# ScalarE issues the stores of the layer-norm stages, SyncE only the loads

## The chip, the core and the metric

The kernel runs on one core of a Trainium2 chip. The metric is the device time of one execution in microseconds (us). Three runs of the kernel before took 9191.78, 9195.85 and 9219.41 us; the median is 9195.85. All data are f32. A core has TensorE (PE), VectorE (DVE), ScalarE (ACT), GpSimd (POOL) and SyncE (SP), each with its own list of instructions and a sequencer that works through it in order; they wait for each other by semaphores. 16 DMA engines move data between HBM and the on-chip memories.

## The reference, cut to what matters

A graph network in four layers over 50000 nodes of 256 features, with 50000 edges sorted by destination. Each layer adds what its graph operation gives to x and normalises each row:

```python
x = _layernorm(x + _L0_gnn_ref(x, edge_index, edge_weight, L0_gnn_W, L0_gnn_b), axis=-1)
x = _layernorm(x + _L1_gnn_ref(x, ...), axis=-1)   # attention, 8 heads
x = _layernorm(x + _L2_gnn_ref(x, ...), axis=-1)   # attention, 8 heads
x = _layernorm(x + _L3_gnn_ref(x, ...), axis=-1)   # filter, update, batch norm over all nodes, plus x
```

Layer 0 is a two-hop propagation, then relu and a 256 x 256 product. Layers 1 and 2 take softmax-weighted sums over the edges of each destination. Layer 3 has a batch norm over nodes, so its last pass needs the sums of a pass before.

## The kernel before, in words

The nodes are padded to 128 x 392 and laid out so that partition p holds 392 consecutive nodes. A step handles G = 2 columns, that is 2 tiles of 128 rows x 256, and there are NS = 4 buffers of everything; so each phase has 392 / 2 = 196 steps (R = 49 rounds of 4). The program runs twelve phases one after the other: setup, hop_edges, hop_nodes, hop_edges, layer_nodes(0), attention_edges(1), layer_nodes(1), attention_edges(2), layer_nodes(2), filter_edges, update_nodes, finish_nodes. The layer-norm stages are layer_nodes(0), (1), (2) and finish_nodes.

In layer_nodes GpSimd gathers the sums of each node from HBM (L717, two indirect DMAs a step). SyncE loads x (L688), in layer 0 also the table T (L691). VectorE combines them, adds the bias (L728), adds up to z (L779), takes bn_stats (L613) and bn_aggr (L621), and later the reciprocal (L631) and the shift (L636). ScalarE takes the root (L626), and applies scale and shift to make xo (L642). In layers 0 and 1 TensorE turns xo (psX, L831), ScalarE copies it (L801), TensorE multiplies it by the next layer's weights (psV, L858, one bank for each of the two tiles and no second pair), and ScalarE copies the result into tt (L808, L810), the rows of the next layer's gather table. In layer 0 ScalarE also rectifies (L791), and TensorE has a turn (psR) and a product (psZ, L844) more. The two results go to HBM: xo to X1, X2 or X3 (L696), tt to T1 (L702), in layer 1 to T2 and ET (L704, L705).

In finish_nodes SyncE loads ht (L1346, the transposed output of update_nodes) and x (L1348), ScalarE applies the batch norm (L1379), TensorE turns it back (L1365), VectorE adds x (L1405), and the same norm follows, with xo stored to out (L1352).

The order on each engine is written out by unrolled(rounds, slots, stages): at time t it calls every stage of its list, in the order of the list, for step t minus the stage's lag. On SyncE load has lag 0, store lag APPLY + 2 and store_table lag TABLE + 2 (TABLE = APPLY + 2; APPLY is 4 in layer 0, else 2); in finish_nodes load has 0 and store 5. On ScalarE the root has lag ADD (3 in layer 0, else 1), apply has APPLY = ADD + 1, the copy of the turned tile APPLY + 1 and the table rows TABLE. hold(e, sem, value) puts a wait in the engine's list; on SyncE, GpSimd and ScalarE it stands as an instruction of its own. A load holds for the buffers' last readers four steps back (mixed and biased; in layer 0 turned for T; in finish_nodes turned for ht and summed for x). A store holds for the semaphore of what it stores (normed, evened, finished). apply and the table rows hold for the store four steps back (stored, stored_t).

Of the kernel before, what the change touches and what calls it, by code (L numbers as in the profile page):

```python
# [24 lines left out]
SW = VW + H  # L25
TW = SW + H
# [17 lines left out]
def signal(stage, s):  # L44

    sems, _, dmas = stage
    return sems[s if dmas else 0]


def done(stage, i, s, back=0):  # L50

    sems, slots, dmas = stage
    if dmas:
        return sems[(s - back) % slots], (i + ((s - back) // slots + 1)) * (16 * dmas)
    return sems[0], i * slots + (s - back + 1)


def total(stage, rounds):

    sems, slots, dmas = stage  # L60
    return [(sem, rounds * (16 * dmas if dmas else slots)) for sem in sems]


def unrolled(rounds, slots, stages):

    for t in range(rounds * slots + max(lag for _, lag in stages)):
        for stage, lag in stages:
            if 0 <= t - lag < rounds * slots:
                stage((t - lag) // slots, (t - lag) % slots)


def build(nc, N, x, src, srcT, dst, dst_next, ew, rbfT, attr3T, attr64T, w0T, b0, w1T, w1, a1, encW, bias1,
# [28 lines left out]
    def hold(e, sem, value):  # L101


        if isinstance(value, int) and value <= 0:
            return
        e.wait_ge(sem, value)
        if e.engine in alone:
            e.sem_inc(marks, 1)  # L108
# [4 lines left out]
    def nodes(t):  # L113
        return t[0:NP, :].rearrange("(p c) d -> p c d", p=P)
# [3 lines left out]
    T1, T2, ET = dram("T1", NP, TW), dram("T2", NP, SW), dram("ET", NP, H)  # L118
# [4 lines left out]
    with ExitStack() as keep:  # L123
# [524 lines left out]
        def layer_nodes(layer):  # L648

            xin = x if layer == 0 else nodes((X1, X2)[layer - 1])  # L650
            xout = nodes((X1, X2, X3)[layer])
            table = layer < 2
            with ExitStack() as ctx:
                G, NS = 2, 4
                R = C // (G * NS)
# [5 lines left out]
                xT, tt = (tiles("xT", D), tiles("tt", TW)) if table else (None, None)  # L661
# [18 lines left out]
                with nc.Block() as block:  # L680
                    @block.sync
                    def _(e):

                        def load(i, s):
                            c = bass.ds(i * (G * NS) + s * G, G)
                            hold(e, *done(st_["mixed"], i, s, NS))
                            hold(e, *done(st_["biased"], i, s, NS))
                            e.dma_start(xt[s][:], xin[:, c, :]).then_inc(signal(loaded, s), 16)  # L688
                            if layer == 0:
                                hold(e, *done(st_["turned"], i, s, NS))  # L690
                                e.dma_start(yt[s][:], nodes(T)[:, c, :]).then_inc(signal(loaded, s), 16)  # L691

                        def store(i, s):
                            c = bass.ds(i * (G * NS) + s * G, G)
                            hold(e, *done(st_["normed"], i, s))
                            e.dma_start(xout[:, c, :], xo[s][:]).then_inc(signal(stored, s), 16)  # L696

                        def store_table(i, s):
                            c = bass.ds(i * (G * NS) + s * G, G)
                            hold(e, *done(st_["evened"], i, s))  # L700
                            if layer == 0:
                                e.dma_start(nodes(T1)[:, c, :], tt[s][:]).then_inc(signal(stored_t, s), 16)  # L702
                            else:
                                e.dma_start(nodes(T2)[:, c, :], tt[s][:, :, 0:SW]).then_inc(signal(stored_t, s), 16)  # L704
                                e.dma_start(nodes(ET)[:, c, :], tt[s][:, :, SW:TW]).then_inc(signal(stored_t, s), 16)  # L705

                        unrolled(R, NS, [(load, 0), (store, APPLY + 2)] + ([(store_table, TABLE + 2)] if table else []))
                        for sem, value in total(stored, R) + (total(stored_t, R) if table else []):
                            e.wait_ge(sem, value)

                    @block.gpsimd
                    def _(e):
# [74 lines left out]
                    @block.scalar  # L787
                    def _(e):
                        def rectify(i, s):
                            hold(e, *done(st_["mixed"], i, s))  # L790
                            e.activation(yt[s][:], yt[s][:], ACT.Relu, scale=0.5).then_inc(signal(st_["rectified"], s), 1)  # L791

                        def copy_turned(i, s):
                            hold(e, *done(st_["turned"], i, s))
                            hold(e, *done(st_["product"], i, s, NS))
                            e.copy(rT[s][:].rearrange("p g d -> p (g d)"), psR[s % 2][:]).then_inc(signal(st_["copied"], s), 1)

                        def copy_turned_x(i, s):
                            hold(e, *done(st_["turnedx"], i, s))
                            hold(e, *done(st_["tabled"], i, s, NS))  # L800
                            e.copy(xT[s][:].rearrange("p g d -> p (g d)"), psX[s % 2][:]).then_inc(signal(st_["copiedx"], s), 1)  # L801

                        def tabled_rows(i, s):

                            hold(e, *done(st_["tabled"], i, s))
                            hold(e, *done(stored_t, i, s, NS))
                            for k in range(G):
                                e.copy(tt[s][:, k, 0:VW].rearrange("p (h w) -> p h w", h=H)[:, :, 0:HD],  # L808
                                       psV[k][:, 0:D].rearrange("p (h d) -> p h d", h=H))
                                ins = e.copy(tt[s][:, k, VW:TW], psV[k][:, D:DW])  # L810
                            ins.then_inc(signal(st_["evened"], s), 1)

                        def apply(i, s):
                            hold(e, *done(stored, i, s, NS))
                            if table:
                                hold(e, *done(st_["turnedx"], i, s, NS))
                            ln_apply(e, i, s, st_["normed"])

                        stages = [(rectify, 0), (copy_turned, TURN)] if layer == 0 else []
                        stages += [(lambda i, s: ln_root(e, i, s), ADD), (apply, APPLY)]  # L820
                        if table:
                            stages += [(copy_turned_x, TURNX), (tabled_rows, TABLE)]
                            e.wait_ge(ones, 1)
                        unrolled(R, NS, stages)

                    @block.tensor
                    def _(e):
# [499 lines left out]
        def finish_nodes():  # L1327
            with ExitStack() as ctx:
# [11 lines left out]
                with nc.Block() as block:  # L1340
                    @block.sync
                    def _(e):

                        def load(i, s):
                            hold(e, *done(turned, i, s, NS))
                            e.dma_start(ht[s][:], HT[:, :, bass.ds(i * (G * NS * P) + s * (G * P), G * P)]).then_inc(signal(loaded, s), 16)  # L1346
                            hold(e, *done(summed, i, s, NS))
                            e.dma_start(xt[s][:], nodes(X3)[:, bass.ds(i * (G * NS) + s * G, G), :]).then_inc(signal(loaded, s), 16)  # L1348

                        def store(i, s):  # L1350
                            hold(e, *done(finished, i, s))
                            e.dma_start(out[:, bass.ds(i * (G * NS) + s * G, G), :], xo[s][:]).then_inc(signal(stored, s), 16)  # L1352

                        unrolled(R, NS, [(load, 0), (store, 5)])
                        for sem, value in total(stored, R):
                            e.wait_ge(sem, value)

                    @block.tensor
                    def _(e):
# [10 lines left out]
                    @block.scalar  # L1370
                    def _(e):
                        e.wait_ge(agged, 1)
                        e.activation(sd[:, :, 0], mv[:, :, 1], ACT.Sqrt, bias=epsc[:]).then_inc(rooted, 1)
                        e.wait_ge(scaled, 4)

                        def batch_norm(i, s):
                            hold(e, *done(loaded, i, s))
                            for m in range(K):
                                ins = e.activation(ht[s][:, m, :], ht[s][:, m, :], ACT.Identity, bias=shift[:, m, :], scale=scale[:, m, :])  # L1379
                            ins.then_inc(signal(normed, s), 1)  # L1380

                        def apply(i, s):
                            hold(e, *done(stored, i, s, NS))
                            ln_apply(e, i, s, finished)

                        unrolled(R, NS, [(batch_norm, 0), (lambda i, s: ln_root(e, i, s), 2), (apply, 3)])

                    @block.vector
                    def _(e):
# [77 lines left out]
```

## Time and profile before

| | us |
|---|---|
| median of 3 runs | 9195.85 |
| profiled execution | 9210.81 |
| its span, first to last instruction | 9209.1 |
| TensorE busy | 4799.2 (52%) |
| VectorE busy | 6234.8 (68%) |
| ScalarE busy | 3278.4 (36%) |
| GpSimd busy | 5451.7 (59%) |
| layer_nodes(0), 1962 to 2876 | 914 |
| layer_nodes(1), 4057 to 4835 | 778 |
| layer_nodes(2), 5890 to 6492 | 602 |
| finish_nodes, 8663 to the end | 546 |

The shares are over the whole span, and the phases have different limits, so what an engine does in one phase is to be read from that phase. PE is TensorE's matmuls, PEld its weight loads; the ends of matmuls are modelled, so their starts tell more. SPq is SyncE's sequencer with its DMA issues. "[1.79 <-DMA xt<-X]" behind an instruction is the idle time of its engine just before, and what ended it. The DMA share is the mean busy share of the 16 DMA engines.

### The profile page before, as it was taken

The page shows a single profiled execution, that of the slowest core. Times are in us where ns is not written, and L with a number is a line of the kernel's source. Part 1 is how long each engine was busy: PE and PEld are TensorE (multiplying, and loading weights), DVE is VectorE, ACT ScalarE, POOL GpSimd, SP SyncE. Part 2 cuts the span into 40 slices and gives each one's busy share as a digit, 9 for nine tenths or more (in the row PEclk, how much of TensorE's full clock was granted, in tenths as well). Part 3 has the DMA queues.
Part 4 walks back from the last instruction along what each step waited for, and adds up shares of the span by engine and source line. Part 5 has one row for each costly group of instructions (what it writes and reads, how often), then busy time and mean ns, then how long its engine had stood idle before and what let it go on. Part 6 is the DMA issues. An engine that isn't in the chain of part 4 may idle for free. (4 is left out here: it accounts for less than half of the span.)

```text
span 9209.1 us, 103278 instructions
## 1 busy us (share of the span) xinstructions
PE 4799.2 (52%) x18908; PEld 3452.2 (37%) x18908; DVE 6234.8 (68%) x20123; ACT 3278.4 (36%) x8442; POOL 5451.7 (59%) x5121
## 2 busy tenths in 40 slices
PE   8856000039996333347771111100688887899743
PEld 4422000038884211225551111100455555788622
DVE  7899333358887999977777777799544444455566
ACT  4433002347774111126660000144222222344588
POOL 7877777764445666655547777677788888100000
PEclk9999555569997555569995555555777778899855
DMA  0299899989886445459984444588544444566688
GB/s 20 99 344 338 284 309 297 309 274 299 297 294 195 146 146 148 147 173 285 278 268 117 122 122 123 165 266 266 108 79 79 79 79 79 165 200 199 214 292 284
DMA packets 1143019, 1839.84 MB, mean 200 GB/s; under 512 B 218094, under 2 KB 564898, under 8 KB 1142374
## 3 DMA queue, kind: packets, MB, share of 16 engines
q1 hardware_dynamic: 884838, 1245.79, 39.8%
q0 software_dynamic: 257536, 587.44, 26.3%
q14 instruction: 483, 3.96, 0.1%
q8 instruction: 162, 2.65, 0.1%
HBM read 1044.55 MB, written 788.03 MB: 199 GB/s over the span
## 5 line engine op out<-in xcount | busy, mean ns | idle before, releaser
L717 POOL DMA_INDIRECT st<-S,last_i x1176 | 1325.6, 1127 | 897.6 <-DVE yt L759 370.4
L915 POOL DMA_INDIRECT rows<-T,src_i x784 | 800.8, 1021 | 251.1 <-issue 248.1
L642 ACT ACTIVATE xo<-z,shift,rsd 128x256 f32<-128x256 f32 x1568 | 851.0, 591 | 1.3 <-issue 1.1
L1128 POOL DMA_INDIRECT A<-comb,ai x392 | 702.5, 1792 | 159.6 <-issue 145.0
L931 PE MATMUL psE<-encs,attr 4*128 4x256 f32 x784 | 404.9, 668 | 745.2 <-DMA attr<-in_attr3T 745.2
L946 ACT ACTIVATE ex<-diff 128x32 f32<-128x32 f32 x392 | 89.8, 229 | 1709.6 <-DVE diff L993 1709.6
L1200 DVE TENSOR_SCALAR eq<-psI,src_f 128x128 f32<-128x128 f32 x392 | 136.7, 349 | 743.2 <-DMA A<-comb,ai 708.4
L931 PE MATMUL psE<-fes,attr 64*128 64x8 f32 x784 | 199.5, 363 | 821.7 <-DMA attr<-in_attr64T 819.4
L477 DVE SCALAR_TENSOR_TENSOR sums<-sums,same,rows 128x256 f32<-128x256 f32 x784 | 380.2, 485 | 326.6 <-ACT rows L458 312.4
L1142 PE MATMUL psH<-rbf,wf1s 20*128 20x256 f32 x784 | 278.9, 485 | 613.9 <-DMA rbf<-in_rbfT 613.9
L931 PEld LDWEIGHTS psE<-encs,attr 4*128 4x128 f32 x784 | 227.5, 319 | 922.3 <-DMA attr<-in_attr3T 884.7
L613 DVE BATCH_NORM_STATS2 row_stats<-z 128x6 f32<-128x256 f32 x1568 | 560.6, 399 | 0.1
L913 POOL DMA_INDIRECT rowsd<-T,dst_i x392 | 384.1, 980 | 266.3 <-DVE sums L1010 150.3
L543 PE MATMUL psC<-sums,chain 128*128 128x256 f32 x4 | 2.4, 699 | 1034.9 <-PEq L417 1034.9
L1156 PE MATMUL psF<-wf2s,hid 128*128 128x256 f32 x1568 | 522.2, 494 | 0.0
L858 PE MATMUL psV<-w2s,xT 128*128 128x272 f32 x1568 | 436.5, 424 | 122.5 <-ACT tt L810 122.5
L931 PEld LDWEIGHTS psE<-fes,attr 64*128 64x128 f32 x784 | 181.2, 319 | 840.4 <-DMA attr<-in_attr64T 838.0
L458 ACT ACTIVATE rows<-rows,w_next 128x256 f32<-128x256 f32 x392 | 177.6, 500 | 850.8 <-DMA rows<-T,src_i 850.8
L445 POOL DMA_INDIRECT rows<-in_x,src_i x392 | 375.6, 958 | 170.0 <-issue 151.8
L1121 POOL DMA_INDIRECT rows<-X,dst_i x392 | 391.3, 998 | 135.9 <-issue 119.1
L913 POOL DMA_INDIRECT rowsd<-ET,dst_i x392 | 376.9, 962 | 150.3 <-issue 119.2
L445 POOL DMA_INDIRECT rows<-T,src_i x392 | 382.1, 975 | 127.7 <-issue 101.2
(232 smaller groups left out, 15612.8 us busy)
## 6 DMA issues: line engine op xcount, KB each, us to landing
X<-xo SPq DMA_DIRECT2D x588, 256.0 KB
xt<-X SPq DMA_DIRECT2D x588, 256.0 KB
S<-sums SPq DMA_DIRECT2D x392, 272.0 KB, 2.4
A<-zero SPq DMA_DIRECT2D x392, 256.0 KB, 4.8
S<-sums SPq DMA_DIRECT2D x392, 256.0 KB, 4.1
xt<-in_x SPq DMA_DIRECT2D x392, 256.0 KB
T<-tt SPq DMA_DIRECT2D x196, 280.0 KB
T<-tt SPq DMA_DIRECT2D x196, 272.0 KB
```

Of the source, the lines that this page charges most:

```text
L445: e.indirect_dma_start(rows[s][:, k, :], None, table, bass.IndirectOffsetOnAxis(ap=src_i[:, c:c + 1], axis=0))\
L477: ins = e.scalar_tensor_tensor(sums[s][:, k, 0:D], last, same[:, bass.ds(i * (G * NS) + (s * G + k), 1)], rows[s][:, k, :], ALU.mult, ALU.add)
L613: ins = e.bn_stats(row_stats[s][:, k, :], z[s][:, k, :])
L642: ins = e.activation(y[s][:, k, :], z[s][:, k, :], ACT.Identity, bias=shift[s][:, k, :], scale=rsd[s][:, k, :])
L717: e.indirect_dma_start(st[s][:, k, :], None, sums_table, bass.IndirectOffsetOnAxis(ap=last_i[:, c:c + 1], axis=0))\
L858: mm = e.matmul(psV[k][:, 0:DW], xT[s][:, k, m * P:(m + 1) * P], weights[:, m, :], start=m == 0, stop=m == K - 1)
L913: e.indirect_dma_start(rowsd[s][:, k, :], None, dtable, bass.IndirectOffsetOnAxis(ap=dst_i[:, c:c + 1], axis=0))\
L915: e.indirect_dma_start(rows[s][:, k, :], None, table, bass.IndirectOffsetOnAxis(ap=src_i[:, c:c + 1], axis=0))\
L931: mm = e.matmul(psE[s % 2][:, k * EW:(k + 1) * EW], attr[s][:, k, :], weights[:], start=True, stop=True)
L1121: e.indirect_dma_start(rows[s][:, k, :], None, X3, bass.IndirectOffsetOnAxis(ap=dst_i[:, c:c + 1], axis=0))\
L1128: e.indirect_dma_start(A[k], bass.IndirectOffsetOnAxis(ap=ai[s][:, k, :], axis=0), comb[s][:, k, :], None, compute_op=ALU.add).then_inc(si ...
L1156: mm = e.matmul(psF[s % 2][:, k * D:(k + 1) * D], hid[s][:, m, k * P:(k + 1) * P], wf2s[:, m, :], start=m == 0, stop=m == K - 1)
```

## The change

The stores and their closing waits move from SyncE's list to ScalarE's. On ScalarE, store has lag APPLY + 1 and stands behind apply, and store_table has lag TABLE + 1 and stands behind the table rows; in finish_nodes store has lag 4 and stands behind apply (lag 3). What a store waits for was thus made by ScalarE in its iteration before. SyncE keeps the loads with their waits. The numbers of DMAs, their sizes, buffers and semaphores are the same.

```diff
 # layer_nodes, block.sync
-                        def store(i, s):
-                            c = bass.ds(i * (G * NS) + s * G, G)
-                            hold(e, *done(st_["normed"], i, s))
-                            e.dma_start(xout[:, c, :], xo[s][:]).then_inc(signal(stored, s), 16)
-
-                        def store_table(i, s):
...
-                        unrolled(R, NS, [(load, 0), (store, APPLY + 2)] + ([(store_table, TABLE + 2)] if table else []))
-                        for sem, value in total(stored, R) + (total(stored_t, R) if table else []):
-                            e.wait_ge(sem, value)
+                        unrolled(R, NS, [(load, 0)])
 # layer_nodes, block.scalar
+                        def store(i, s):
+                            c = bass.ds(i * (G * NS) + s * G, G)
+                            hold(e, *done(st_["normed"], i, s))
+                            e.dma_start(xout[:, c, :], xo[s][:]).then_inc(signal(stored, s), 16)
+
+                        def store_table(i, s):
+                            c = bass.ds(i * (G * NS) + s * G, G)
+                            hold(e, *done(st_["evened"], i, s))
+                            if layer == 0:
+                                e.dma_start(nodes(T1)[:, c, :], tt[s][:]).then_inc(signal(stored_t, s), 16)
+                            else:
+                                e.dma_start(nodes(T2)[:, c, :], tt[s][:, :, 0:SW]).then_inc(signal(stored_t, s), 16)
+                                e.dma_start(nodes(ET)[:, c, :], tt[s][:, :, SW:TW]).then_inc(signal(stored_t, s), 16)
+
                         stages = [(rectify, 0), (copy_turned, TURN)] if layer == 0 else []
-                        stages += [(lambda i, s: ln_root(e, i, s), ADD), (apply, APPLY)]
+                        stages += [(lambda i, s: ln_root(e, i, s), ADD), (apply, APPLY), (store, APPLY + 1)]
                         if table:
-                            stages += [(copy_turned_x, TURNX), (tabled_rows, TABLE)]
+                            stages += [(copy_turned_x, TURNX), (tabled_rows, TABLE), (store_table, TABLE + 1)]
                             e.wait_ge(ones, 1)
                         unrolled(R, NS, stages)
+                        for sem, value in total(stored, R) + (total(stored_t, R) if table else []):
+                            e.wait_ge(sem, value)
 # finish_nodes, block.sync
-                        unrolled(R, NS, [(load, 0), (store, 5)])
+                        unrolled(R, NS, [(load, 0)])
 # finish_nodes, block.scalar
-                        unrolled(R, NS, [(batch_norm, 0), (lambda i, s: ln_root(e, i, s), 2), (apply, 3)])
+                        unrolled(R, NS, [(batch_norm, 0), (lambda i, s: ln_root(e, i, s), 2), (apply, 3), (store, 4)])
+                        for sem, value in total(stored, R):
+                            e.wait_ge(sem, value)
```

## Rows read from the trace of the kernel before

**Rows 1.** Windows of the four stages: us, busy per engine, PEclk, DMA share, GB/s

```profile
1962.00:2876.00 914.00, 885.52 (x4704) 750.41 (x4704) 753.46 (x2356) 679.48 (x1960) 432.01 (x393) 0.99 0.87 288
4057.00:4835.00 778.00, 550.20 (x2352) 393.85 (x2352) 584.90 (x2156) 503.53 (x1566) 428.02 (x391) 0.94 0.90 275
5890.00:6492.00 602.00, 0.00 (x0) 0.00 (x0) 580.19 (x2156) 255.88 (x589) 462.60 (x390) 0.50 0.84 261
8663.00:9209.10 546.10, 218.36 (x784) 140.29 (x784) 344.96 (x1378) 437.82 (x982) 0.00 (x0) 0.50 0.86 283
```

**Rows 2.** SyncE's waits over the whole span: total us, times, longest

```profile
SPq L108 <- ACT xo L642: 1135.7, 734, 7.6
...
SPq L108 <- ACT tt L810: 361.3, 389, 2.8
...
SPq L108 <- DVE z L766: 13.4, 2, 7.0
```

**Rows 3.** Groups by line, in 4200:4700 and in 8750:9150 (columns as in the page)

```profile
L728 DVE TENSOR_TENSOR xb<-xt,b1s 128x512 f32<-128x512 f32 x128 | 88.7, 693 | 119.4 <-DMA xt<-X 118.8
...
L1379 ACT ACTIVATE ht<-ht,shift,scale 128x256 f32<-128x256 f32 x296 | 160.7, 590 | 70.5 <-DMA xt<-X 69.5
```

**Rows 4.** Windows inside two stages, and one outside (columns as in rows 1)

```profile
460.00:690.00 230.00, 136.46 (x345) 58.49 (x346) 213.93 (x690) 78.04 (x174) 163.83 (x171) 1.00 1.01 344
4200.00:4700.00 500.00, 359.99 (x1534) 258.15 (x1534) 381.49 (x1408) 327.47 (x1023) 279.55 (x255) 0.95 0.91 279
8750.00:9150.00 400.00, 165.24 (x595) 106.06 (x593) 251.85 (x1038) 329.51 (x742) 0.00 (x0) 0.50 0.89 292
```

**Rows 5.** Timeline in layer_nodes(1): start us, us, engine, line, operation

```profile
4401.97 0.20 ACT L810 COPY tt<-psV 128x16 f32<-128x16 f32 x1
...
4402.25 0.37 SPq L704 DMA_DIRECT2D T<-tt  x1
...
4402.31 2.07 PE L858 MATMUL psV<-w2s,xT 128*128 128x272 f32 x8 [0.60 <-ACT tt L810]
...
4402.67 0.47 SPq L705 DMA_DIRECT2D ET<-tt  x1
...
4403.33 0.35 SPq L688 DMA_DIRECT2D xt<-X  x1
...
4405.53 2.07 PE L858 MATMUL psV<-w2s,xT 128*128 128x272 f32 x8 [0.72 <-ACT tt L810]
...
4407.49 0.69 DVE L728 TENSOR_TENSOR xb<-xt,b1s 128x512 f32<-128x512 f32 x1 [1.79 <-DMA xt<-X]
```

**Rows 6.** Timeline in finish_nodes: SyncE's issues and ScalarE

```profile
9042.79 1.07 ACT L1379 ACTIVATE ht<-ht,shift,scale 128x256 f32<-128x256 f32 x2
...
9042.97 0.34 SPq L1352 DMA_DIRECT2D out<-xo  x1
...
9044.05 0.54 SPq L1348 DMA_DIRECT2D xt<-X  x1
...
9045.05 1.09 ACT L1379 ACTIVATE ht<-ht,shift,scale 128x256 f32<-128x256 f32 x2
...
9046.05 0.28 ACT L626 ACTIVATE sd<-mean_var,epsc 128x2 f32<-128x2 f32 x1
...
9046.23 1.08 ACT L642 ACTIVATE xo<-z,shift,rsd 128x256 f32<-128x256 f32 x2
...
9048.19 1.09 ACT L1379 ACTIVATE ht<-ht,shift,scale 128x256 f32<-128x256 f32 x2 [0.88 <-DMA xt<-X]
```

**Rows 7.** Timeline in layer_nodes(0), TensorE: one group in two steps

```profile
2402.45 0.60 PE L831 MATMUL psR<-ident,yt 128*128 128x128 f32 x4
...
2406.89 0.60 PE L831 MATMUL psR<-ident,yt 128*128 128x128 f32 x4
```

**Rows 8.** DMA issues of the page: count, KB each, median us from issue to landing

```profile
out<-xo SPq DMA_DIRECT2D x196, 256.0 KB, 3.4
...
st<-S,last_i POOLq DMA_INDIRECT x1568, 4.5
```

More of the change, by code:

```diff
@@ L691, in load @@
                                 e.dma_start(yt[s][:], nodes(T)[:, c, :]).then_inc(signal(loaded, s), 16)
-                        def store(i, s):
-                            c = bass.ds(i * (G * NS) + s * G, G)
-                            hold(e, *done(st_["normed"], i, s))
-                            e.dma_start(xout[:, c, :], xo[s][:]).then_inc(signal(stored, s), 16)
-                        def store_table(i, s):
[L699 to L705, printed above, removed]
-                        unrolled(R, NS, [(load, 0), (store, APPLY + 2)] + ([(store_table, TABLE + 2)] if table else []))
-                        for sem, value in total(stored, R) + (total(stored_t, R) if table else []):
-                            e.wait_ge(sem, value)
+                        unrolled(R, NS, [(load, 0)])
                     @block.gpsimd
@@ L1348, in load @@
                             e.dma_start(xt[s][:], nodes(X3)[:, bass.ds(i * (G * NS) + s * G, G), :]).then_inc(signal(loaded, s), 16)
-                        def store(i, s):
-                            hold(e, *done(finished, i, s))
-                            e.dma_start(out[:, bass.ds(i * (G * NS) + s * G, G), :], xo[s][:]).then_inc(signal(stored, s), 16)
-                        unrolled(R, NS, [(load, 0), (store, 5)])
-                        for sem, value in total(stored, R):
-                            e.wait_ge(sem, value)
+                        unrolled(R, NS, [(load, 0)])
                     @block.tensor
@@ L1384, in apply, with store @@
                             ln_apply(e, i, s, finished)
-                        unrolled(R, NS, [(batch_norm, 0), (lambda i, s: ln_root(e, i, s), 2), (apply, 3)])
+                        def store(i, s):
+                            hold(e, *done(finished, i, s))
+                            e.dma_start(out[:, bass.ds(i * (G * NS) + s * G, G), :], xo[s][:]).then_inc(signal(stored, s), 16)
+                        unrolled(R, NS, [(batch_norm, 0), (lambda i, s: ln_root(e, i, s), 2), (apply, 3), (store, 4)])
+                        for sem, value in total(stored, R):
+                            e.wait_ge(sem, value)
                     @block.vector
```

## The prediction

> **What bounds the kernel now.** I read the times of the four changed stages first, then whom SyncE's queue waits for, then one step of each stage in order of time. The changed stages, called 0, 1, 2 and final here, take 914, 778, 602 and 546 us [rows 1], 2840 of the 9209 us; the other eight phases stay as they are. Each stage has 196 steps of two 128-row tiles.
>
> SyncE's waits say who holds the loads back [rows 2]: 1135.7 us in all for ScalarE's normalised tile and 361.3 for its table rows. For what an x load itself needs in stages 1 and 2 (the add to z that frees its buffer, L766) it waits twice in all, 13.4 us, once a stage, in the fill. So the buffer is free long before; the load stands in the queue behind a store whose data is not made yet. That costs where the load is then late. In 500 us of stage 1 (128 steps, 3.906 us each) VectorE idles 118.8 us for the x tile; in 400 us of the final stage (296 activations, so 148 steps, 2.703 each) ScalarE idles 69.5 us for its loads [rows 3].
>
> Stage 1, one step [rows 5]. ScalarE's last table copy ends at 4402.17; SyncE issues the two table stores (0.37 and 0.47 us), and the load at 4403.33; VectorE can use it at 4407.49, 4.16 us after. By the queue's order the load of step t+1 stands behind the table store of step t-6, which ScalarE makes in its iteration t-2 (the table rows lag by 4), so the way round spans three steps: copy to load issue 1.16, load 4.16, VectorE's iteration 381.49/128 = 2.98 [rows 4], ScalarE's iteration about 3.2 (the pitch of TensorE's psV, to which its copies keep). That is 11.5 us, 3.83 a step, and measured is 3.906. The stall is this loop.
>
> The final stage is a loop of the same kind [rows 6]: the out store is issued at 9042.97, the xt load behind it at 9044.05, and ScalarE starts on it at 9048.19. With 2.27 us for its iteration that is 7.5 us for three steps here; on the mean 8.1. When its loads are there a step takes 2.26 (9042.79 to 9045.05).
>
> Stage 0 is another case: TensorE starts its group psR at 2402.45 and 2406.89 [rows 7], 4.44 us apart, and it is busy 885.5 of 914 us [rows 1]. 196 x 4.44 = 870, the rest is fill and drain. TensorE is the bound, and the buffers make up for a late load. In stage 2 VectorE is busy 580.2 of 602 us [rows 1]; no load or store touches that.
>
> **The change, part by part.**
> *SyncE loses the stores*: 588 X stores, 196 table stores in stage 0 and 392 in stage 1, 196 of out, each 0.34 to 0.47 us of issue [rows 5, 6], and their waits. Now a load follows its own buffer. In stage 1 that is VectorE's mix of four steps back: four periods less one VectorE iteration, 4 x 3.3 - 3 = 10 us, for 4.2 us of flight. In the final stage xt waits for the add of four steps back, which comes after TensorE's turn and the root of another step, by the code some 3.5 us into that ScalarE iteration: 4 x 2.26 - 3.5 = 5.5 us for the 4.1 of flight. Enough, if flights don't grow much.
>
> *What is late next in stage 1.* TensorE's psV starts at 4402.31 and 4405.53, both times as ScalarE's copies out of the same banks end [rows 5]: 3.22 us a step. The other bound is the DMA engines, share 0.91 at 279 GB/s [rows 4]. As these transfers are, they need 0.91 x 3.906 = 3.55 us a step. The window 460:690 shows share 1.01 and 344 GB/s with another mix of sizes; at that rate the 279 x 3.906 = 1090 KB of a step take 3.17. So the new step ends between 3.22 and 3.55, if all goes, and 3.906, if nothing does. I take 3.4, and 0.1 for lateness that stays: (3.906 - 3.5) x 196 = 80 us; bounds 0 and 134.
>
> *The final stage.* ScalarE's floor is 2.26. DMA as it is: 0.89 x 2.703 = 2.40; at 344 GB/s 789 KB take 2.29. With both so near to each other, and xt's slack short, I take the upper one: (2.70 - 2.40) x 196 = 59 us; bounds 0 and 87.
>
> *Stages 0 and 2.* Stage 0 has 914 - 870 = 44 us besides TensorE's pace, most of it fill and drain (the pipeline is nine steps deep in the table store): 8 us. Stage 2 has 22 us besides VectorE's work, part of it loads: 8. Bounds for the two together 0 and 25.
>
> *ScalarE gains the stores*: one a step in stage 2 and the final one, two in stage 0, three in stage 1, each with a wait on its own step before (long there) and a mark. The trace before has no DMA issued on ScalarE. By SyncE's rows an issue is 0.34, 0.37 and 0.47 us. The two ends: nothing, if the sequencer is ahead of its engine, or all of it. For ahead: the output activation stands behind waits that follow the root in the list, and yet starts at 9046.23, before the root that started at 9046.05 with 0.28 us is over [rows 6]; so the waits were read while the engine worked. The X and out stores stand behind two activations of 1.08 us together, which hide 0.34. In stage 1 the two table stores (0.84, with waits about 1.05) stand behind table copies that I put at 0.8 of the 3.22 - 2.07 = 1.15 us between two psV groups, so 0.25 us shows. ScalarE's other work of a step, 327.47/128 = 2.56 [rows 4] less 0.8, is 1.8, and with 0.25 it fits into psV's 2.07, by a hair. I take nothing for the issues; the row that shows the sequencer ahead is nearest.
>
> The Trainium skill speaks against this cover. "Perfetto Trace Analysis", DMA Instruction — HWDGE, has the issuing sequencer itself wait, have the descriptors made, and only then be free for its next instruction. No row before shows ScalarE in that state. By that rule and with no work queued ahead, the sum would be that of the rival "issue shows".
>
> *A store goes out later*: behind the next activation pair, up to one step. Its buffer is wanted again four steps on, so three are left, 3 x 2.26 = 6.8 us in the final stage, for 3.4 us to landing [rows 8]. Nothing.
>
> Sum: 80 + 59 + 8 + 8 = 155. The profiled execution took 9210.8 (span 9209.1), so 9056; the median of the runs, 9195.85, is 15 lower, so 9041.
>
> **The rivals.**
> *Next wait in line (0.17).* With the loads early VectorE waits for the gathers: two of about 1.1 us on GpSimd (279.55/255 [rows 4]) plus 4.5 to landing [rows 8] plus a VectorE iteration, about 10 us for four periods of 3.2 to 3.5. Against it: 3 us of slack, and no idle for st in stage 1 now. For it: DMA engines near full make flights longer. Stage 1 then stays near 3.75, 31 us: 31 + 59 + 16 = 106, time 9090.
>
> *DMA is at its limit now (0.12).* The share is 0.84 to 0.90 in all four stages [rows 1]; if that is what a mix of loads, stores and gathers yields, a deeper prefetch only lengthens flights. Against it: 1.01 is reached elsewhere [rows 4]. Gain 16 from stages 0 and 2 or less: 9180. The Trainium skill says it in "DMA: Bandwidth & Descriptors", Issuing engines are not separate DMA queues: DMAs of several issuers share the same 16 DMA engines, and only issue time is saved. Rows 2 show waiting, which that sentence leaves out.
>
> *Issue shows, slower (0.09).* If ScalarE stands still while it issues, stage 1 needs 2.56 + 1.18 (0.34, 0.37, 0.47) + 0.35 for waits = 4.1 a step, 0.2 x 196 = +39. Final: 329.51/148 = 2.23 + 0.34 + 0.1 = 2.67, and part of the load wait stays, +15. Stage 0: 679.48/196 = 3.47 + 0.68 + 0.2 = 4.35 of 4.44, TensorE sometimes unfed, +6. Sum +60: 9255. It decides from 1.34 us a step in stage 1, ScalarE's idle time now.
>
> *All floors reached (0.07).* 3.22, 2.26, 4.44: 134 + 86 + 8 + 12 = 240, time 8956.
>
> **How the numbers follow.** The forecast has 0.55, its own range is 9000 to 9085. The range for 8 in 10 is 8970 to 9185: it holds the forecast, the next wait and the DMA rival's middle, not the slower case. A difference under 0.3% (28 us) can't be told from none. Faster: 0.55 + 0.17 + 0.07 = 0.79; same: 0.12; slower: 0.09.
>
> **What would show it.** After the change: SyncE waits for VectorE and TensorE (mix, z, psN) alone; VectorE's idle for xt in stage 1 is under 20 us in 500, ScalarE's in the final stage under 30 in 400; the DMA share is 0.95 or more in both; stages 0 and 2 are within 15 us of 914 and 602; ScalarE has no idle time ended by "issue". It is wrong if stage 1 stays over 3.8 a step with xt early, if activations beside a store start 0.3 us or more after their inputs, or if the DMA share stays at 0.90.

## The result and the profile after

The changed kernel takes 8955.74 us (median of 4 runs, 8954.23 to 8959.3); the kernel before took 9193.82 beside it. The ratio is 0.9737, with a 95% interval from 0.9718 to 0.9755. The forecast was 9041 with a range from 8970 to 9185, so the direction was right and the time lies below the range, at the fourth rival ("all floors reached", 8956, given 0.07). The profiled execution has a span of 8952.5 us, 256.6 less than before.

The windows of the four stages, and one inside stage 1 and one inside the final stage, columns as in [rows 1]:

```profile
1960.80:2846.70 885.90, 869.17 (x4680) 746.97 (x4681) 755.87 (x2352) 674.03 (x1947) 488.96 (x392) 0.99 0.91 295
4034.20:4682.50 648.30, 492.90 (x2331) 375.75 (x2332) 589.78 (x2156) 511.64 (x1556) 476.70 (x392) 0.98 1.01 328
5742.70:6332.00 589.30, 0.00 (x0) 0.00 (x0) 573.18 (x2156) 254.66 (x589) 455.24 (x392) 0.50 0.89 267
8508.00:8952.50 444.50, 218.20 (x784) 140.07 (x784) 336.88 (x1377) 427.09 (x981) 0.00 (x0) 0.50 0.98 343
...
4100.00:4600.00 500.00, 389.00 (x1848) 296.26 (x1847) 462.70 (x1694) 403.53 (x1232) 375.83 (x308) 1.00 1.03 336
8550.00:8900.00 350.00, 176.15 (x633) 112.93 (x632) 268.99 (x1109) 343.91 (x792) 0.00 (x0) 0.50 1.02 357
```

The DMA share of stage 1 has gone from 0.91 to 1.03 and that of the final stage from 0.89 to 1.02 [rows 4]. To compare stages between kernels I take from each trace the time from the start of the first gather to the start of the last output activation, which makes xo (final stage: from the first output activation to the last), and the mean distance of two steps' output activations:

| | stage 0 | stage 1 | stage 2 | final |
|---|---|---|---|---|
| before, us | 899.8 | 770.6 | 602.4 | 523.7 |
| changed, us | 885.3 | 647.8 | 588.7 | 430.5 |
| before, us a step | 4.48 | 3.87 | 3.01 | 2.68 |
| changed, us a step | 4.41 | 3.25 | 2.94 | 2.21 |
| gain forecast, us | 8 | 80 | 8 | 59 |
| gain measured, us | 14.5 | 122.8 | 13.7 | 93.2 |

These are 244 of the 256.6 us. The other 12 lie outside these stretches, at most 6 us in any one place, and I count them as scatter between executions; no run shows what they are.

SyncE's waits after the change, in the form of [rows 2]:

```profile
SPq L108 <- DVE z L750: 1015.3, 384, 7.1
SPq L108 <- PE psR L831: 653.6, 192, 3.5
...
SPq L108 <- PE psN L1359: 184.4, 188, 9.5
...
SPq L108 <- DVE z L1405: 44.6, 184, 0.7
```

The waits for ScalarE's xo and tt are gone. SyncE now waits at nearly every step for the buffer itself: VectorE's use of it in stages 1 and 2, TensorE's transposes in stages 0 and final. These waits are long (1015 us in stages 1 and 2 alone), which is what a loader that is ahead looks like. They cost next to nothing: the groups that answer to [rows 3], in 4100:4600 and 8550:8900, show no idle time for xt in stage 1 and 5.2 us in the final stage.

```profile
L712 DVE TENSOR_TENSOR xb<-xt,b1s 128x512 f32<-128x512 f32 x154 | 105.1, 682 | 0.0
...
L1373 ACT ACTIVATE ht<-ht,shift,scale 128x256 f32<-128x256 f32 x317 | 171.1, 586 | 6.1 <-DMA xt<-X 5.2
```

One step of stage 1 in order of time, ACTq being ScalarE's sequencer:

```profile
4300.34 0.37 ACT L792 COPY tt<-psV 128x256 f32<-128x256 f32 x1
4300.50 0.41 ACTq L814 DMA_DIRECT2D T<-tt  x1
4300.61 0.18 ACT L794 COPY tt<-psV 128x16 f32<-128x16 f32 x1
4300.67 0.39 ACT L792 COPY tt<-psV 128x256 f32<-128x256 f32 x1
4300.94 0.20 ACT L794 COPY tt<-psV 128x16 f32<-128x16 f32 x1
4300.94 0.52 ACTq L815 DMA_DIRECT2D ET<-tt  x1
4301.25 1.67 PEld L858 LDWEIGHTS psV<-w2s,xT 128*128 128x128 f32 x8 [0.91 <-issue]
4301.28 2.07 PE L858 MATMUL psV<-w2s,xT 128*128 128x272 f32 x8 [0.70 <-ACT tt L794]
4301.59 0.30 ACT L626 ACTIVATE sd<-mean_var,epsc 128x2 f32<-128x2 f32 x1 [0.45 <-issue]
4301.86 0.60 ACT L642 ACTIVATE xo<-z,shift,rsd 128x256 f32<-128x256 f32 x1
4301.99 0.34 ACTq L806 DMA_DIRECT2D X<-xo  x1
4302.37 0.58 ACT L642 ACTIVATE xo<-z,shift,rsd 128x256 f32<-128x256 f32 x1
...
4304.50 2.07 PE L858 MATMUL psV<-w2s,xT 128*128 128x272 f32 x8 [0.71 <-ACT tt L794]
```

The T store is issued (4300.50 to 4300.91) while the copies of a later step run on ScalarE (4300.34 to 4301.14), and the X store while xo is made. Only the tail of ET sticks out: the root starts 0.45 us after the last copy. psV starts at 4301.28 and 4304.50, again 3.22 us apart, and that is the step that half of the stage keeps to (the middle half of its steps take 3.18 to 3.27 us; the mean is 3.25).

### The profile page after: what moved, and what is told of

The parts are those of the page before. It is cut to its first block and busy times, and to the rows that moved or that the text cites. A ratio compares the mean times of both kernels' runs of the same rounds, so it can differ in the third digit from the quotient of the medians.

```text
span 8952.5 us, 103278 instructions
## 1 busy us (share of the span) xinstructions
PE 4724.6 (53%) x18908; PEld 3435.4 (38%) x18908; DVE 6238.9 (70%) x20123; ACT 3276.4 (37%) x8442; POOL 5545.9 (62%) x5121
## 3 DMA queue, kind: packets, MB, share of 16 engines
q8 instruction: 162, 2.65, 0.1%
## 5 line engine op out<-in xcount | busy, mean ns | idle before, releaser
L701 POOL DMA_INDIRECT st<-S,last_i x1176 | 1421.0, 1208 | 650.3 <-issue 316.4
L915 POOL DMA_INDIRECT rows<-T,src_i x784 | 802.6, 1024 | 251.0 <-issue 248.6
L858 PE MATMUL psV<-w2s,xT 128*128 128x272 f32 x1568 | 407.8, 403 | 136.1 <-ACT tt L794 136.1
L583 POOL DMA_INDIRECT st<-S,last_i x392 | 384.0, 980 | 123.4 <-issue 105.7
```

The lines of the kernel that those rows point to most:

```text
L583: e.indirect_dma_start(st[s][:, k, :], None, S0, bass.IndirectOffsetOnAxis(ap=last_i[:, c:c + 1], axis=0))\
L701: e.indirect_dma_start(st[s][:, k, :], None, sums_table, bass.IndirectOffsetOnAxis(ap=last_i[:, c:c + 1], axis=0))\
L858: mm = e.matmul(psV[k][:, 0:DW], xT[s][:, k, m * P:(m + 1) * P], weights[:, m, :], start=m == 0, stop=m == K - 1)
L915: e.indirect_dma_start(rows[s][:, k, :], None, table, bass.IndirectOffsetOnAxis(ap=src_i[:, c:c + 1], axis=0))\
```

## The experiments

The runs went to three chips. On one, the first chip from here on, the kernel before takes 9213 us and the changed one 8961, close to the 9194 and 8956 of the result; on the two others the kernel before takes 9564 to 9576. The difference lies mainly outside the four stages: the first gather of stage 0 stands at 1956 us on the first chip and at 2148 on another, and between stages 1 and 2 (attention_edges(2)) pass 1060 us on the one and 1230 on the other. Yet stage 1 of the changed kernel too is 648 us on the first and 667 to 675 on the others. Its steps there keep their middle (3.23 us for 3.22), but more of them are long: a twentieth take over 4.5 us in c1, over 3.8 in c2 on the first chip. Stages 0 and 2 and the final one agree within some 5 us. So a run is compared with those on the same chip, and each ratio is to the kernel before on that chip. The kernel before was profiled in the trace of the prediction alone. An estimate for the chip of e1 to e7: what these runs spend outside the four stages (6755 to 6782 us), taken from the kernel before beside them, leaves 2784 to 2809 us for its stages, where the trace of the prediction has 2797; so its stage times are used there too. The table has the stages in us as above; each comes from one profiled execution.

| run | ratio, 95% | stage 0 | 1 | 2 | final |
|---|---|---|---|---|---|
| changed (c1) | 0.9756 (0.9736 to 0.9776) | 884.8 | 675.0 | 591.6 | 431.2 |
| e1 waits only | 0.9967 (0.9952 to 0.9983) | 901.4 | 736.3 | 604.3 | 528.2 |
| e2 late on SyncE | 0.9747 (0.9730 to 0.9763) | 884.4 | 665.4 | 594.1 | 419.9 |
| e3 one step later | 0.9755 (0.9736 to 0.9775) | 884.7 | 685.5 | 583.3 | 426.5 |
| e4 tables on SyncE | 0.9921 (0.9904 to 0.9937) | 902.1 | 770.8 | 590.2 | 433.5 |
| e5 two pairs | 0.9777 (0.9761 to 0.9794) | 885.2 | 681.4 | 589.8 | 431.0 |
| e6 one extra | 0.9773 (0.9753 to 0.9792) | 884.9 | 686.5 | 591.8 | 432.8 |
| e7 three extra | 1.0004 (0.9992 to 1.0017) | 886.5 | 812.3 | 597.2 | 501.9 |
| changed (c2), first chip | 0.9721 (0.9708 to 0.9734) | 884.1 | 648.2 | 588.1 | 434.3 |
| e11 final late on SyncE | 0.9708 (0.9694 to 0.9721) | 885.4 | 647.9 | 590.1 | 423.0 |
| e9 less moved | 0.971, one run | 884.9 | 648.1 | 592.3 | 419.7 |
| e10 less moved, two pairs | 0.968, one run | 884.5 | 591.8 | 590.9 | 433.9 |
| changed (c3), third chip | 0.9770 (0.9756 to 0.9784) | 884.8 | 667.3 | 593.3 | 430.7 |
| e13 two pairs again | 0.9796 (0.9781 to 0.9811) | 884.8 | 686.8 | 594.9 | 433.1 |
| e12 pairs and final | 0.9793 (0.9775 to 0.9810) | 885.2 | 684.6 | 595.7 | 422.6 |

**Is it the place of the waits?** e1 is the changed kernel, and SyncE waits as before, without issuing:

```diff
-                        unrolled(R, NS, [(load, 0)])
+                        def await_store(i, s):
+                            hold(e, *done(st_["normed"], i, s))
+
+                        def await_table(i, s):
+                            hold(e, *done(st_["evened"], i, s))
+
+                        unrolled(R, NS, [(load, 0), (await_store, APPLY + 2)] + ([(await_table, TABLE + 2)] if table else []))
```

and in the final stage (await_store, 5) on finished. 

> The changed kernel, with the stores on ScalarE, but SyncE's list gets back the waits that its stores had (for normed, evened and finished, at the old lags) without issuing anything there. Theory (the loads stood behind waits): the old loop is back, less some 1 us of issue out of three steps in stage 1, so stage 1 about 3.6 to 3.8 us a step, the final stage 2.5 to 2.65, the whole 9110 to 9180 us. Rival (what helped is a second issuer with a queue of its own): stays at 8956, 3.25 and 2.2 us a step.

Measured: stages 0, 2 and final are back at 901, 604 and 528 us, the values before. The final stage's 2.71 us a step lies above the 2.5 to 2.65 expected: it got back all of the old loss (2.68), although SyncE issues a DMA less a step. Stage 1 is at 736, 3.70 us a step. Two rows of this kernel, SyncE's waits and the group of the bias add in 550 us:

```profile
SPq L108 <- ACT xo L642: 1131.8, 578, 8.0
```

```profile
L718 DVE TENSOR_TENSOR xb<-xt,b1s 128x512 f32<-128x512 f32 x148 | 102.4, 692 | 105.2 <-DMA xt<-X 81.6 <-issue 23.0
```

The waits alone, with every store on ScalarE, make the loads late again. In stage 1 a part stays gained (3.70 for 3.87). I put it down to the table stores' 0.84 us of issue, which is no longer in a way round of three steps (that would be 0.28 a step, and 0.17 came); no run separates it. The whole time, 9535, is above the 9180 of the expectation because the chip is another; its ratio of 0.9967 is 9163 us where the kernel before takes 9194.

e2 keeps all DMAs on SyncE and raises only the stores' lags:

```diff
-                        unrolled(R, NS, [(load, 0), (store, APPLY + 2)] + ([(store_table, TABLE + 2)] if table else []))
+                        unrolled(R, NS, [(load, 0), (store, APPLY + 5)] + ([(store_table, TABLE + 5)] if table else []))
...
-                        unrolled(R, NS, [(load, 0), (store, 5)])
+                        unrolled(R, NS, [(load, 0), (store, 7)])
```

> The kernel before, all DMAs on SyncE, only the lags of its stores raised: store APPLY+2 to APPLY+5, store_table TABLE+2 to TABLE+5, in the final stage 5 to 7, so that what a store waits for is long made when the list comes to it. Theory (the place of the waits): 8950 to 8990 us, stage 1 near 3.25 a step, the final stage 2.2 to 2.3. Rival (a second issuer and queue are needed, SyncE's issue time or its one queue limits): over 9100.

Measured: 0.9747, the changed kernel's ratio (0.9756 beside it, c1). The final stage takes 2.15 us a step, better than the 2.2 to 2.3 expected. The same group now never idles:

```profile
L728 DVE TENSOR_TENSOR xb<-xt,b1s 128x512 f32<-128x512 f32 x166 | 113.1, 681 | 0.0
```

So neither a second issuer nor its queue is needed. Only the loads must not stand behind waits for work that is later than they are. e3 does the same with one step more of lag (APPLY + 3, TABLE + 3, 6). 

> The kernel before, all DMAs on SyncE, its stores only one step later: lags APPLY+3, TABLE+3 and 6 for APPLY+2, TABLE+2 and 5. Theory (a loop that spans a number of steps): the way round of 11.5 us in stage 1 spans four steps and not three, 2.9 a step, so something else is the bound already, 3.3 to 3.4; the final stage 8.1/4 = 2.0, so 2.15 to 2.2. Almost the whole gain, ratio 0.972 to 0.978. Rival (each step of lag takes off its share): stage 1 about 3.6, ratio near 0.985.

Measured: 0.9755, as good as c1 in the whole. Stage 1 takes 3.44 us a step, just over the 3.3 to 3.4 expected, and 685.5 us for c1's 675.0: VectorE still idles 33.4 us in 550 for xt. So one step just suffices, as a way round over four steps in place of three makes it.

e4 leaves the table stores on SyncE at TABLE + 2 and the X and out stores on ScalarE. 

> The changed kernel, but the table stores (T1, T2, ET) stay on SyncE at their old lag; the X and out stores are on ScalarE. Theory: the loop of stage 1 goes through the table rows, so stage 1 stays at 3.7 to 3.9 us a step; stage 2 and the final stage keep their gain (14 and 93 us); the whole 9070 to 9090. Rival (each store moved gives its share): stage 1 about 3.55, the whole near 9020.

Measured: stages 0 and 1 at 902 and 771 us, their times before; 2 and final at 590 and 434, as changed. VectorE waits for x in stage 1 again, in 550 us:

```profile
L723 DVE TENSOR_TENSOR xb<-xt,b1s 128x512 f32<-128x512 f32 x143 | 99.0, 693 | 125.2 <-DMA xt<-X 113.8 <-issue 10.9
```

Moving the X store alone gives stage 1 nothing: the way round goes through the table rows. Whether moving the table stores alone would give all of it was not run. The whole gained less than expected: 0.9921 (0.9904 to 0.9937), where 9070 to 9090 us would be 0.987 to 0.989. The stages of the profiled run, the fastest of four, account for 100 us of gain, the medians for 75; the rest stays open.

**Does ScalarE pay for issuing?** c1 is the changed kernel on the chip of these runs. 

> The changed kernel once more, on the chip of the runs beside it, as their base. Ratio to before 0.97 to 0.98; stage 0 about 885 us, stage 1 about 648, stage 2 about 589, the final stage 2.2 us a step. If stage 1 takes 665 us or more here, the slower stage 1 of the run with two pairs of psV banks was the chip and not the banks.

Its stage 1 is 675 us, so most of what e5 (two pairs of psV banks, below: 681 us) showed beside 648 was the chip. e6 adds to each X and out store a small one:

```diff
                             e.dma_start(xout[:, c, :], xo[s][:]).then_inc(signal(stored, s), 16)
+                            for j in range(1):
+                                e.dma_start(nodes(SPARE[layer * 1 + j])[:, i * (G * NS) + s * G, :], zero[:, 0:H]).then_inc(spared, 16)
```

> The changed kernel with one more DMA a step on ScalarE behind each X and out store: 128 rows of 32 bytes of zeros to a spare table, 4 KB, no wait. Theory (issue runs beside ScalarE's engine, and there is room in its sequencer): stages 0, 2 and final within 1% of the changed kernel; stage 1, where the issues already hold back the root by 0.45 us a step, 3.3 to 3.5 a step for 3.25. Rival (issue shows): about 0.3 us a step in every stage but 2, some 180 us.

Measured: stages 0, 2 and final unchanged (432.8 for 431.2 us in the final stage), stage 1 686.5 for 675.0, 3.44 us a step as expected. e7 has range(3). 

> As the run with one extra DMA, but three more a step (about 1 us of issue). Theory: the sequencer of ScalarE runs out of room: stage 1 about 4.0 to 4.3 us a step, the final stage 2.15 to 2.6, stage 0 4.5 to 4.8, stage 2 as it was; the whole 200 to 350 us over the changed kernel. Rival (issue never shows beside the engine): under 30 us over it.

Measured: the whole gain is gone (1.0004). Stage 1 takes 4.09 us a step, the final stage 2.57. Stage 0 hides nearly all (886.5 us, 4.41 a step, where 4.5 to 4.8 was expected). ScalarE's groups in 400 us of the final stage:

```profile
L1378 ACT ACTIVATE ht<-ht,shift,scale 128x256 f32<-128x256 f32 x312 | 170.2, 592 | 47.5 <-issue 47.5
```

and one stretch of it in order of time:

```profile
9303.17 0.52 ACTq L1389 DMA_DIRECT2D SPARE<-zero  x1
9303.53 0.58 ACT L643 ACTIVATE xo<-z,shift,rsd 128x256 f32<-128x256 f32 x1
9303.72 0.52 ACTq L1389 DMA_DIRECT2D SPARE<-zero  x1
9304.37 0.60 ACT L1378 ACTIVATE ht<-ht,shift,scale 128x256 f32<-128x256 f32 x1 [0.25 <-issue]
```

So the issues run beside ScalarE's engine, up to a limit. In the final stage one issue more a step (0.82 us of issue in all) fits beside 2.15 us of activations, and three more (1.85 us in all) don't: 0.30 us a step of idle time ended by "issue" (47.5 us in 156 steps). 1.85 is still less than 2.15. I take it that the waits and activations in the sequencer's list, which have no time of their own in the profile, use the rest; no run shows it. The Trainium skill says in "Perfetto Trace Analysis", DMA Instruction — HWDGE, that the sequencer is free for its next instruction only when the issue is done. The trace agrees: the issue at 9303.17 ends at 9303.69, the next starts at 9303.72. What that costs is another matter: the out store's 0.34 us alone are hidden.

**What bounds the stages now?** e9 is the changed kernel without the x loads after the first round, in stage 1 and the final stage; e10 leaves them out in stage 1 alone and has two pairs of psV banks. The outputs of both are not the reference's, and each ran once. The first part of the diff is in both, the rest in e10:

```diff
 # layer_nodes, load on SyncE
+                            if layer == 1 and i:
+                                return
...
 # psV
-                psV = [bank(f"psV{j}", 512) for j in range(2)] if table else None
+                psV = [bank(f"psV{j}", 512) for j in range(4 if layer else 2)] if table else None
+                pairs = 2 if layer else 1
...
-                            hold(e, *done(st_["evened"], i, s, 1))
+                            hold(e, *done(st_["evened"], i, s, pairs))
```

Expected of c2 (the changed kernel beside them), e9 and e10, in this order:

> The changed kernel as the base of the three runs beside it, on their chip. Ratio to before 0.972 to 0.978; the final stage 2.2 us a step, stage 1 between 3.25 and 3.4.

> The changed kernel with the x loads left out after the first round of four steps in stage 1 and in the final stage (so its output is not the reference's): 256 KB a step less, a quarter of stage 1's traffic and a third of the final stage's. If the DMA engines bind (share 1.0), stage 1 falls below 3.2 or steadies, and the final stage below 2.15 us a step. If ScalarE binds the final stage, it stays at 2.15 to 2.2; if TensorE's and ScalarE's cycle binds stage 1, it is 3.22 in nearly every step.

> The changed kernel with two pairs of psV banks and, in stage 1, without the x loads after the first round (its output is not the reference's). If with less moved the psV cycle is what is left (3.22), the second pair now takes it to 2.9 to 3.1 us a step. If GpSimd's gather issue binds (two of 1.2 and 0.3 a step), it stays at 3.0 to 3.2.

Measured, beside c2 (windows 4100:4600, then 8550:8900, of e9; then the first of e10):

```profile
4100.00:4600.00 500.00, 390.78 (x1856) 297.43 (x1855) 464.11 (x1701) 405.81 (x1235) 375.06 (x310) 1.00 0.88 257
8550.00:8900.00 350.00, 181.10 (x650) 116.27 (x651) 276.13 (x1137) 349.57 (x813) 0.00 (x0) 0.50 0.82 244
```

```profile
4100.00:4600.00 500.00, 436.15 (x2040) 316.35 (x2040) 494.55 (x1868) 428.65 (x1359) 392.00 (x341) 1.00 0.93 282
```

With a quarter less to move (257 for 337 GB/s) stage 1 takes 648.1 us for 648.2. The DMA engines do not bind it at a share of 1.03. With the second pair as well it takes 591.8, 2.96 a step, VectorE at 494.6 of 500: the psV cycle (TensorE's product waits until ScalarE has copied the one before out of the same banks) was the bound. In the final stage ScalarE is busy 349.6 of 350 us, and a step is 2.15, its floor. The 2.21 to 2.23 of the changed kernel are 0.06 to 0.08 more; its rows count 5.2 us of idle time for xt in 158 steps, 0.03 a step, and the rest I put down to the same lateness.

With all of the traffic the second pair does not pay. It stands in e5, beside c1; in e13, beside c3; and in e12, which also has the late out store of e11 below. Expected of e5, c3, e13 and e12, in this order:

> The changed kernel with two pairs of psV banks in stage 1 in place of one, so that TensorE's product of a step no longer waits for ScalarE's copies of the step before. If stage 1 (3.25 us a step) is now bound by that cycle of 3.22, it falls to what GpSimd and VectorE need, 3.0 to 3.17, 15 to 40 us off 8956. If it is bound by the DMA engines (share 1.03) or by GpSimd's gathers, it stays within 10 us.

> The changed kernel as the base of the two runs beside it. Stage 1 about 648 us on one kind of chip, about 675 on the other.

> Two pairs of psV banks in stage 1 with all of the traffic, beside the changed kernel. If the DMA engines can carry a step's 1090 KB in less than 3.22 us, stage 1 falls below the changed kernel's, to 3.05 to 3.2 us a step (10 to 40 us off). If their bound is about 3.25 (share 1.03 now), stage 1 stays within 8 us of it.

> Two pairs of psV banks and the final stage's store late on SyncE. Expected: the sum of the two, 10 us for the final stage plus what the run beside it gains in stage 1; 8905 to 8950 where the changed kernel takes 8960.

Measured: stage 1 at 681 us beside 675, and 687 and 685 beside 667; the ratios are 0.9777 beside 0.9756, and 0.9796 and 0.9793 beside 0.9770. No gain came in any of the three. e5's 6 us more is inside the 10 that was to speak for the DMA engines or the gathers as the bound, which e9 and e10 contradict on the first chip; e13's 20 us more fits neither of its two cases; e12 was to gain and takes 30 us more in the median, though its final stage gained 8 us. The steps no longer have 3.22 us each: in e13 a twentieth are under 2.35 and a twentieth over 5.9. The group of the table copies in 500 us, c3 and then e13:

```profile
L792 ACT COPY tt<-psV 128x256 f32<-128x256 f32 x302 | 109.2, 382 | 28.9 <-PE psV L858 11.5 <-DMA srow<-PARTS 5.7 <-issue 5.3
```

```profile
L793 ACT COPY tt<-psV 128x256 f32<-128x256 f32 x292 | 105.1, 380 | 81.3 <-PE psV L859 43.7 <-DMA srow<-PARTS 28.1 <-issue 9.0
```

In this place the only DMA that the copies wait for is the table store of four steps before (the name in the row is of an earlier phase's tensor). So, as I read it, the steps bunch and then stand for stores in flight; that this makes the stage slower is argued from these rows and not shown. Why it makes the mean longer, and whether it would on the first chip, where this was not run, stays open.

**A better version.** e11 is the changed kernel with the out store of the final stage back on SyncE, (store, 7). 

> The changed kernel, but in the final stage the out store is back on SyncE, with lag 7 in place of 5; the layer stages are as changed. The run with all stores late on SyncE had 420 us from the first to the last output activation there, the changed kernel 431. Expected 10 us under the changed kernel beside it (0.1%), if it is the stores' place that makes the difference; none if it was chance.

Measured: 8948.90 us (8945.01 to 8950.61) beside 8960.67 (8952.18 to 8964.26), 11.8 us less, and the final stage 423.0 for 434.3 us. It is the best kernel of this study with the right output, by 0.13%. ScalarE idles 1.7 us in 8550:8900 for xt, beside 8.3 in c2. e12 shows the same 423 us for the final stage on another chip, beside 431 (c3). So the out store costs some 10 us more on ScalarE than late on SyncE; most of it shows in the rows as waits for x and none as issue, and why x comes later stays open.

## Why the prediction was wrong, by its steps

- **SyncE's loads stand behind stores**: right. e1 and e2 show it from both sides, and e4 that stage 1's way round goes by the table rows, as [rows 5] were read; in stage 0 too the gain goes by them (902 us in e4).
- **The loop of three steps**: right in kind. e3's one step more takes it away.
- **Stage 1, "I take 3.4, and 0.1 for lateness that stays"**: this is the term that failed; 3.25 came out, 123 us for 80. It is half of the 85 us by which the forecast was off. The lower bound of 3.22 [rows 5] was the answer. The upper, 0.91 x 3.906 = 3.55 us of DMA work, was none. Two shares of queues, 4200:4700 before (x128 steps) and 4100:4600 after (x154 steps), show why; q0 are the gathers, q1 and q10 the rest:

```profile
q1 hardware_dynamic: 106366, 103.63, 63.2%
q0 software_dynamic: 12258, 35.57, 27.8%
```

```profile
q10 hardware_dynamic: 105594, 84.31, 50.9%
q0 software_dynamic: 14780, 42.90, 26.9%
q1 hardware_dynamic: 22162, 40.36, 24.8%
```

  Loads and stores took 0.632 x 3.906 = 2.47 us a step before and (0.509 + 0.248) x 3.247 = 2.46 after. The gathers took 1.09 before and 0.87 after, with the same bytes. So a gather's busy time is not fixed by its bytes. I read the part that shrank with the step as waiting; the rows show only that it shrank. And e9 shows that even 1.03 was no bound.
- **The final stage, "I take the upper one"**: the same error, 93 us for 59. 0.89 x 2.703 = 2.41 us of share became 1.02 x 2.21 = 2.25. ScalarE's floor was the bound, 2.15 and not 2.26: I had read a step with a short wait in it, and the one before it took 2.17 (9040.62 to 9042.79). e2 keeps to 2.15 with all of the traffic, at a share of 1.03.
- **Stages 0 and 2**: 14.5 and 13.7 us for 8 and 8. In stage 0 the reading was wrong: the 4.44 of [rows 7] was one pair of steps and not the pace. Before, nine steps in ten took 3.8 to 6.0 us, 4.48 in the mean; now most take 4.44, 4.41 in the mean. The 44 us "besides TensorE's pace" were partly such late steps, and 0.075 us a step is the whole gain; the time from the first gather to the first output activation stayed at 25 us. In stage 2 VectorE's 2.91 is reached in most steps.
- **Issues on ScalarE cost nothing**: right within some 10 us, wrong in one sign to look for. ScalarE idles 71.2 us in 500 ended by "issue" in stage 1, 0.46 a step for the 0.25 that I put; psV's 2.07 us cover it, for the step is still psV's 3.22. The out store's place costs the 10 us of e11, and in stage 1 e2, with no store on ScalarE, takes 665 us beside c1's 675, one trace of each.
- **Next wait in line, the gathers**: VectorE idled 0.3 us in 500 for st. The rival is refuted on the chip of the prediction.
- **DMA is already the limit**: refuted. The Trainium skill says in "DMA: Bandwidth & Descriptors", Issuing engines are not separate DMA queues, that DMAs of several issuers run on the same 16 engines and save only the time of the issue. e2 agrees: with one issuer it comes to 0.9747, c1 with two to 0.9756. What was to be had was the idle tenth of the share, and the rule doesn't speak of that.
- **The range** ended at 8970 because I left the 0.07 of "all floors reached" outside it. It should have reached the floors, since nothing in the trace but the DMA share stood against them. That this rival's 8956 is the measured time is in part luck: its 134 us for stage 1 (122.8 came) and 86, 8 and 12 for the final stage and stages 0 and 2 (93.2, 14.5 and 13.7 came) are off by 11 us one way and 15 the other.

## What to carry to other kernels

Read a queue's waits by what they wait for: when a loading queue waits for later stages' results and hardly ever for a free buffer, its loads are held by their place in the list. Here raising the stores' lag by a step or more gave the same as a second issuing engine, so try that first, and give a second engine no more issues than its compute covers. To size such a gain, count from the floors of the compute engines and their cycles; a DMA share below 1 times the period was no floor here.

## What the runs showed of the hardware

The busy share of the 16 DMA engines reached 1.03, and stage 1 took as long with it as with 0.88 (e9, one run). The same kernel (the one before) took 9213 us on one chip and 9564 to 9576 on two others. Of the changed kernel's four stages only stage 1 was clearly longer there (667 to 675 us for 648), though stages 0 and 2 have the same gathers. An issue on ScalarE took 0.33 to 0.38 us for the X, out and T stores and 0.55 in the mean for ET, beside the running activation; on SyncE the same stores took 0.32 to 0.38 and 0.50.
